# Where the block sums of V are made and turned, in an attention and expert kernel

## Chip, cores and metric

The kernel runs on one core of one Trainium2 chip. The metric is the device time of one execution in microseconds. A core has five engines with instruction streams of their own: TensorE (PE, with its weight loads as PEld), VectorE (DVE), ScalarE (ACT), GpSimd (POOL) and SyncE (SP, which issues most DMAs here). They meet only at semaphores.

## What is computed

The input x has 8 batches of 512 tokens with 256 features. It is layer-normalised to xn, and the output is x + attention(xn) + experts(xn). All is float32. The attention, cut to its core (16 heads, 16 features each):

```python
q, k, v = (xn @ Wq.T, xn @ Wk.T, xn @ Wv.T)      # split into 16 heads
qf, kf = taylor_exp(q), taylor_exp(k)            # [1, x / 16**.25, (x outer x) / (sqrt(2) * 4)]
A = jnp.tril(jnp.einsum('bhnd,bhmd->bhnm', qf, kf))
y = jnp.einsum('bhnm,bhme->bhne', A, v)
z = 1.0 / (jnp.einsum('bhld,bhld->bhl', qf, jnp.cumsum(kf, axis=2)) + EPS)
return (y * z[..., None]).reshape(b, l, 256) @ Wo.T
```

The experts are 8 feed-forward nets (256 to 512 and back, silu gate), of which each token uses the best two.

## The kernel before

**Scores.** With s = q.k, the score qf.kf is 1 + s/4 + s*s/32, which is ((s/4 + 1)^2 + 1) / 2. So TensorE makes s, and ScalarE makes the square (0.25 s + 1)^2 (`squares0`, `squares1`, `squares2`, lines 520 to 540). The 1 that is still to be added under the square gives, for a query, the sum of V over all keys up to it. The kernel gets it in two parts: inside a block of 128 tokens GpSimd masks the square with a fill of -1 (`mask`, line 476), and for blocks as a whole TensorE adds up V: that is the step C (lines 1088 to 1097), whose sums ScalarE copies to Cs (562) and TensorE turns (transposes) to columns, the step T (1098 to 1100); VectorE keeps them in CT (766) and adds them to each quad's product in `copy_yw` (719). V has a 17th column of ones, which gives the denominator in the same way.

**Quads.** The attention runs over 32 quads n = 4b + qd: batch b, four heads each. A quad has three parts of scores, and TensorE's program around them (lines 1149 to 1160) stands below with the lists. `attend(n - 1)` is the product of the last quad's squares with V (line 1056), made behind the first scores of this quad. `slot_a`, `slot_b` and `slot_c` (42 to 75) are lists written out by hand of the other steps that TensorE takes behind the first scores and the product, behind the second scores, and behind the third; ScalarE and VectorE walk the same lists for their share of each step. The steps:

- ("x", b, j): turn of xn (line 1067); ("c", b, k): a q product for k = 0 and 2 or a k product for k = 1 and 3 (1076), the "third q product" being c with k = 2, the q of quads 2 and 3 of the batch; ("v", b, j): V and router logits (1085)
- ("C", b, 0): block sums; ("T", b, 0): their turn
- ("t", b, qd): turn of a quad's product (1105), which VectorE then divides (`normalise`, 722 to 735, three instructions, the last of which, yn at 733, releases the bank)
- ("y", b, k): turn of yn (1111), k = 1 of which needs the t of quads 2 and 3; ("o", b, k): product with Wo (1120); ("r", b, 0): ranks of tokens for the experts (1125, 1127); ("f", ...): filler.

**Banks.** All these steps share three PSUM banks in rotation. `misc_uses` gives bank i % 3 to the i-th step of the whole list, and TensorE's `free` waits before a step until the step three places ahead of it in the list has been released by its last reader:

```python
    for i, key in enumerate(steps + list(END)):
        used[i % 3] += 1
        table[key] = (i % 3, used[i % 3])
```

For c with k = 2 the last reader is VectorE (744): ScalarE first copies the product to the high part of Q2 (553), then VectorE subtracts that copy from the bank for the low part and releases it. For c with k = 3 ScalarE copies K2 (555) and VectorE makes Kt (752). For y ScalarE copies yTh (568), VectorE makes yTl (775). For C the release is ScalarE's copy of Cs, for T VectorE's copy of CT.

**VectorE's order.** In its loop (959 to 973) a quad has copy_yw, the steps of slot_a, `before_b`, the steps of slot_b, `after_b`, the steps of slot_c, `after_c`. Line 966 puts the c of slot_b last on VectorE in quads 0 and 2, other than in the last batch. For quad 0 `before_b` is the gates of the experts, `after_b` the norm of the next batch's x.

**Moves.** The low and high parts of q and k go to other partitions by DMAs: `move_q` and `move_k` on SP's queue (lines 308 to 320, 349 to 365), four DMAs each, in a fixed order. The moves of q for quads 2 and 3 of a batch wait for c with k = 2, those of k behind them for c with k = 3. The scores of quads 2 and 3 wait for them (1029, 1030).

After quad 31 the expert stage runs 71 tiles of 128 gathered tokens (from line 1166).

Of the kernel before, what the change touches and what calls it, by code (L numbers as in the profile page):

```python
# [21 lines left out]
LAST = NBATCH - 1  # L22
# [18 lines left out]

def slot_a(n):

    return [("C", 0, 0)] if n == 0 else []


def slot_b(n):

    b, qd = divmod(n, 4)
    if qd == 0:  # L50
        steps = [("T", b, 0), ("c", b, 2)]
    elif b == LAST:
        steps = [("o", b - 1, qd - 1)] if qd < 3 else []
    elif qd == 1:
        steps = [("x", b + 1, 0), ("x", b + 1, 1)]
    elif qd == 2:
        steps = [("c", b + 1, 1)]
    else:
        steps = [("o", b - 1, 0)] if b else []
    if n == NQ - 1:  # L60
        steps.append(("f", n, 7))
    return steps + ([("t", (n - 1) // 4, (n - 1) % 4)] if n else []) + ([("G", 0, 0)] if n == NQ - 1 else [])


def slot_c(n):


    b, qd = divmod(n, 4)
    if qd == 0:
        return [("c", b, 3)] + ([("y", b - 1, 1)] if b else []) + [("r", b, 0)]  # L70
    if b == LAST:
        return [("y", b, 0)] if qd == 3 else [("f", n, 9)]
    if qd == 3:
        return ([("o", b - 1, 1)] if b else []) + [("y", b, 0), ("C", b + 1, 0)]
    return ([("c", b + 1, 0)] if qd == 1 else []) + [("v", b + 1, 2 * qd - 2), ("v", b + 1, 2 * qd - 1)]


# [35 lines left out]
def build(nc, x, wqk, wv, wo, w12, w3, out):  # L113
    with ExitStack() as ctx:
# [541 lines left out]
        def vector_program(e):  # L656
# [57 lines left out]
            def copy_yw(n):  # L714
                e.wait_ge(s["p_av"], n + 1)
                if n >= 2:
                    e.wait_ge(s["p_t"], n - 1)
                done(e, "T", n // 4, 0)
                e.tensor_tensor(yw[n % 2].rearrange("p (i m) -> p i m", i=4), banks[:, 4, :].rearrange("p (i m) -> p i m", i=4),
                                CT[:, n % 4, :].unsqueeze(2).to_broadcast([P, 4, P]), ALU.add).then_inc(s["v_yw"], 1)  # L720
# [199 lines left out]
            def after_b(n):  # L920
                b, qd = divmod(n, 4)
                if n == NQ - 3:
                    tile_starts()
                elif n == NQ - 2:
                    tile_rows(1)
                elif n == NQ - 1:
                    expert_ends()
                elif n == 0:
                    gates(0)
                elif qd == 0 and b < LAST:  # L930
                    norm_x(b + 1)
                elif qd == 1 and b < LAST:
                    place_rows(b)
                if n == NQ - 2:
                    w12_low(8)
# [23 lines left out]
            for n in range(NQ):  # L959
                if n:  # L960
                    copy_yw(n - 1)
                for item in slot_a(n):
                    step(*item)
                before_b(n)
                items = slot_b(n)
                if n % 4 in (0, 2) and n // 4 < LAST:
                    items = [i for i in items if i[0] != "c"] + [i for i in items if i[0] == "c"]
                for item in items:
                    step(*item)
                after_b(n)  # L970
                for item in slot_c(n):
                    step(*item)
                after_c(n)
# [265 lines left out]
        with nc.Block() as block:  # L1239
            block.sync(sync_program)  # L1240
            block.gpsimd(gpsimd_program)
            block.scalar(scalar_program)
            block.vector(vector_program)
            block.tensor(tensor_program)
# [34 lines left out]
```

## Time and profile before

| | |
|---|---|
| median of 3 runs | 668.18 us (668.07 to 668.24) |
| span of the profiled execution | 665.4 us |
| own time of the profiled execution | not listed, only its span |
| TensorE busy | 641.8 us, 96% |
| VectorE, ScalarE, GpSimd busy | 410.6, 341.6, 344.1 us |
| quads of the attention | about 20 to 301 us |

The span runs from the first to the last instruction; the run's time has some microseconds around it. "Busy" of TensorE means that a matmul was in flight. The granted clock is what the chip allowed TensorE, in tenths of full speed (2.4 GHz).

In a timeline each row has the start and the length in us, the engine, the line of the code, the instruction with out<-in, its shape and count, and in brackets the idle time before it with what ended it. Neighbouring matmuls overlap in their rows, since each row counts until its results have left the array.

### The profile page before, as it was taken

To read this page: it belongs to the slowest core of one execution; us is meant where nothing else is said; L and a number is where in the kernel's file an instruction comes from. 1 tells how busy PE (TensorE), PEld (TensorE's weight loads), DVE (VectorE), ACT (ScalarE), POOL (GpSimd) and SP (SyncE) were. 2 spreads that over 40 slices of the span, in tenths; PEclk is the share of its full clock that TensorE was granted. 3 is DMA by queue.
4 is the path that set the end of the run, shared out by engine and by line. 5 is a ranking of instruction groups with operands and counts; after the bars stand their busy time and mean duration, and the time that the engine had idled before them with its cause. 6 is when DMAs were issued, how large, how long until landed. Compare 5 with 4: busy or idle time off the path is not lost.

```text
span 665.4 us, 16423 instructions
## 1 busy us (share of the span) xinstructions
PE 641.8 (96%) x5414; PEld 496.5 (75%) x5414; DVE 410.6 (62%) x1067; ACT 341.6 (51%) x515; POOL 344.1 (52%) x381
## 2 busy tenths in 40 slices
PE   8899999999999999999999999999999999999994
PEld 7555666666666666657888888888888888888883
DVE  6777788787878585777975444444544445444452
ACT  3668878787877686766642232322323223232331
POOL 3265655546463736473465555455545555455542
PEclk9999999999999999999999999999999999999998
DMA  4653555554443435447633434333333433333332
GB/s 134 141 133 99 127 153 130 152 130 147 93 136 77 128 85 154 118 150 249 207 59 58 66 51 66 50 57 60 58 59 50 66 51 57 58 51 58 58 50 25
DMA packets 37775, 64.07 MB, mean 96 GB/s; under 512 B 8289, under 2 KB 25825, under 8 KB 37697
## 3 DMA queue, kind: packets, MB, share of 16 engines
q0 software_dynamic: 16704, 28.12, 22.0%
q1 hardware_dynamic: 20432, 34.24, 20.2%
q8 instruction: 50, 0.82, 0.5%
q10 hardware_dynamic: 560, 0.66, 0.3%
q14 instruction: 29, 0.23, 0.1%
HBM read 27.72 MB, written 22.68 MB: 76 GB/s over the span
## 4 chain that ended last, share of the span: by engine, by line
PE 87%; DVE 4%; DMA 2%; ACT 2%; issue 2%; SPq 1%; ACTq 0%; POOL 0%; POOLq 0%; DVEq 0%
PE banks L1182 29%; PE banks L1203 15%; PE banks L1056 10%; PE banks L1038 8%; PE banks L1076 7%; PE banks L1191 5%; PE banks L1085 4%; PE banks L1120 3%; PE banks L1171 2%; PE banks L1105 1%; PE banks L1111 1%; DMA K<-Kt 1%; ACT T L533 1%; DVE xTl L740 1%; PE banks L1094 1%
## 5 line engine op out<-in xcount | busy, mean ns | idle before, releaser
L496 POOL DMA_INDIRECT out<-yo,xw x71 | 112.2, 1581 | 154.4 <-DVE yo L996 76.6
L625 ACT ACTIVATE sTh<-banks 128x512 fp32r<-128x512 f32 x71 | 42.5, 598 | 192.4 <-PE banks L1191 186.6
L476 POOL TENSOR_SCALAR_AFFINE_SELECT T<-T 128x512 f32<-128x512 f32 x128 | 80.8, 642 | 108.5 <-ACT T L539 43.1
L988 DVE TENSOR_TENSOR sTl<-banks,sTh 128x512 fp32r<-128x512 f32 x71 | 49.0, 691 | 118.9 <-ACT sTh L625 118.9
L1182 PE MATMUL banks<-w12h,xgh 128*128 x284 | 118.0, 415 | 0.6 <-DVE xgl L979 0.6
L1182 PE MATMUL banks<-w12l,xgh 128*128 x284 | 112.2, 395 | 0.0
L1182 PE MATMUL banks<-w12h,xgl 128*128 x284 | 112.1, 395 | 0.0
L485 POOL DMA_INDIRECT xg<-xs_scr,glist x71 | 72.4, 1020 | 21.5 <-issue 20.0
L1056 PE MATMUL banks<-T,vau 128*17 128x512 f32 (+3 forms) x1024 | 75.6, 434 | 0.9 <-POOL T L476 0.9
L467 POOL DMA_INDIRECT xs_scr<-xb,slots x64 | 64.3, 1004 | 18.7 <-issue 10.0
L1038 PE MATMUL banks<-Q,K 32*128 32x256 f32 (+2 forms) x1024 | 70.5, 358 | 3.5 <-DMA K<-Kt 2.2
L525 ACT ACTIVATE T<-banks 128x1024 f32<-128x1024 f32 x64 | 62.1, 1026 | 12.5 <-PE banks L1038 11.9
L533 ACT ACTIVATE T<-banks 128x768 f32<-128x768 f32 x64 | 48.5, 810 | 27.2 <-PE banks L1038 27.2
L1182 PEld LDWEIGHTS banks<-w12h,xgl 128*128 128x128 f32 x284 | 53.3, 188 | 12.0
L1056 PEld LDWEIGHTS banks<-T,vau 128*17 128x17 f32 x1024 | 26.0, 97 | 46.3 <-issue 38.4
L1182 PEld LDWEIGHTS banks<-w12h,xgh 128*128 128x128 f32 x284 | 53.8, 189 | 7.8 <-issue 1.0
L1038 PEld LDWEIGHTS banks<-Q,K 32*128 32x128 f32 x1024 | 38.6, 183 | 27.1 <-ACT T L525 12.7
L1182 PEld LDWEIGHTS banks<-w12l,xgh 128*128 128x128 f32 x284 | 53.9, 190 | 6.3
L996 DVE TENSOR_SCALAR yo<-banks,xw 128x256 f32<-128x256 f32 x71 | 34.3, 483 | 39.0 <-PE banks L1203 31.2
L539 ACT ACTIVATE T<-banks 128x768 f32<-128x768 f32 x64 | 48.7, 810 | 18.0 <-PE banks L1038 16.1
L1009 DVE TENSOR_TENSOR hs<-banks,hs 128x512 f32<-128x512 f32 x71 | 49.1, 692 | 10.2 <-PE banks L1182 0.9
L1203 PE MATMUL banks<-w3h,sTh 128*128 x284 | 51.1, 302 | 0.8 <-ACT sTh L625 0.8
(174 smaller groups left out, 1222.3 us busy)
## 6 DMA issues: line engine op xcount, KB each, us to landing
Q<-Q SPq DMA_DIRECT2D x128, 64.0 KB, 2.4
w12r<-w SPq DMA_DIRECT2D x16, 512.0 KB, 4.2
out<-xa SPq DMA_DIRECT2D x16, 256.0 KB
w3r<-w SPq DMA_DIRECT2D x8, 512.0 KB, 8.7
K<-Kt SPq DMA_DIRECT2D x124, 32.0 KB
xa<-x SPq DMA_DIRECT2D x7, 512.0 KB, 4.7
xg<-xs_scr,glist POOLq DMA_INDIRECT x71
out<-yo,xw POOLq DMA_INDIRECT x71
```

What stands on the lines that cost most here:

```text
L467: e.indirect_dma_start(xs_d, bass.IndirectOffsetOnAxis(slots[:, k, 4 * b + blk:4 * b + blk + 1].bitcast(U32), 0), xb[b % 2][:, blk, :], No ...
L476: e.affine_select(out=v, in_=v, pattern=[[0, 4], [1, P]], compare_op=ALU.is_ge, fill=-1.0, base=0, channel_multiplier=-1).then_inc(s["g_mk ...
L485: e.indirect_dma_start(xg[:, t % GR, :], None, xs_d, bass.IndirectOffsetOnAxis(glist[:, t:t + 1].bitcast(U32), 0)).then_inc(s[f"d_g{t % GR ...
L496: e.indirect_dma_start(out, bass.IndirectOffsetOnAxis(xw[:, t % 4, NE:NE + 1].bitcast(U32), 0), yo[:, t % 2, :], None, compute_op=ALU.add) ...
L525: e.activation(T0[n % 2][:, 2 * h:2 * h + 2, :], banks[:, 2 * h:2 * h + 2, :], ACT.Square, scale=0.25, bias=1.0).then_inc(s["a_s"], 1)
L533: e.activation(T1[:, 2 * h:2 * h + 2, :], banks[:, 2 * h:2 * h + 2, 0:384], ACT.Square, scale=0.25, bias=1.0).then_inc(s["a_s"], 1)
L988: e.tensor_tensor(sTl[:], banks[:, 5, :], sTh[:].bitcast(F32), ALU.subtract).then_inc(s["v_st"], 1)
L1009: e.tensor_tensor(hs[:], banks[:, 2 * (t % 2) + 1, :], hs[:], ALU.mult).then_inc(s["v_mu"], 1)
L1038: i = e.matmul(banks[:, r, c0:c0 + w], K2[rr, g, h, jm * P:(jm + 1) * P], Q2[g][rr, h, p, 512 - w:512], start=(p == 0), stop=(p == 1))
L1056: i = e.matmul(banks[32 * r:32 * r + HA, 4, 512 - w:512], vau[b % 2][:, jm, 4 * qd + r, :], v[:, r, :], start=(jm == 0), stop=(jm == 2), s ...
L1182: i = e.matmul(banks[:, 2 * (t % 2) + m, :], a[:, k, :], w[:, bass.ds(expert[t] * 4 + (2 * k + m), 1), :], start=(k == 0 and n == 0), stop ...
L1203: i = e.matmul(banks[:, 6 + t % 2, 0:256], a[:, k * P:(k + 1) * P], w[:, bass.ds(expert[t] * 4 + k, 1), :], start=(k == 0 and n == 0), sto ...
```

## The change

In slot lists: C of a batch goes from slot_c of the quad before to slot_a of its own quad 0; behind it, c with k = 2 goes ahead of T in slot_b. On VectorE the c of quad 0 is no longer put last. The bank rotation follows the new order by itself. Nothing else is changed.

```diff
 def slot_a(n):
-    return [("C", 0, 0)] if n == 0 else []
+    return [("C", n // 4, 0)] if n % 4 == 0 else []

 def slot_b(n):
     b, qd = divmod(n, 4)
     if qd == 0:
-        steps = [("T", b, 0), ("c", b, 2)]
+        steps = [("c", b, 2), ("T", b, 0)]
...
 def slot_c(n):
...
     if qd == 3:
-        return ([("o", b - 1, 1)] if b else []) + [("y", b, 0), ("C", b + 1, 0)]
+        return ([("o", b - 1, 1)] if b else []) + [("y", b, 0)]
...
                 items = slot_b(n)
-                if n % 4 in (0, 2) and n // 4 < LAST:
+                if n % 4 == 2 and n // 4 < LAST:
                     items = [i for i in items if i[0] != "c"] + [i for i in items if i[0] == "c"]
```

## Rows read from the trace of the kernel before

**Rows 1.** The page: busy time by engine, and TensorE's granted clock in 40 slices
```profile
PE 641.8 (96%) x5414; PEld 496.5 (75%) x5414; DVE 410.6 (62%) x1067; ACT 341.6 (51%) x515; POOL 344.1 (52%) x381
...
PEclk9999999999999999999999999999999999999998
```

**Rows 2.** The list of waits of TensorE: us in total, times, longest us
```profile
engine line waited for: us in total, times, longest us
PE banks L1076 <- DVE xTl L740: 3.6, 7, 0.5
...
PE banks L1038 <- DMA K<-Kt: 2.2, 2, 1.4
```

**Rows 3.** Timeline of TensorE at batch 4: start, length, engine, line, instruction, idle before
```profile
158.46 0.68 PE L1094 MATMUL banks<-vau,below 128*32 128x68 f32 x32
...
159.07 0.74 PE L1038 MATMUL banks<-Q,K 32*128 32x512 f32 x8
...
159.73 2.35 PE L1056 MATMUL banks<-T,vau 128*17 128x512 f32 x32
...
162.01 0.62 PE L1038 MATMUL banks<-Q,K 32*128 32x384 f32 x8
...
162.57 0.33 PE L1100 MATMUL banks<-ident,Cs 128*128 128x128 f32 x1
...
162.65 0.48 PE L1076 MATMUL banks<-xTh,Wqh 128*128 128x512 f32 x1
...
165.33 0.50 PE L1076 MATMUL banks<-xTh,Wqh 128*128 128x512 f32 x1
...
166.59 0.39 PE L1076 MATMUL banks<-xTl,Wqh 128*128 128x512 f32 x1
...
166.87 0.66 PE L1111 MATMUL banks<-ident,yn 128*128 128x128 f32 x4
```

**Rows 4.** Timeline of ScalarE at batch 4
```profile
156.83 1.57 ACT L539 ACTIVATE T<-banks 128x768 f32<-128x768 f32 x2 [1.55 <-PE banks L1038]
...
159.20 0.23 ACT L562 ACTIVATE Cs<-banks 128x68 f32<-128x68 f32 x1
...
159.84 1.94 ACT L525 ACTIVATE T<-banks 128x1024 f32<-128x1024 f32 x2 [0.40 <-PE banks L1038]
...
162.67 1.51 ACT L533 ACTIVATE T<-banks 128x768 f32<-128x768 f32 x2 [0.80 <-PE banks L1038]
...
164.32 1.03 ACT L553 ACTIVATE Q<-banks 128x1024 fp32r<-128x1024 f32 x1
```

**Rows 5.** Timeline of VectorE at batch 4
```profile
165.60 1.21 DVE L744 TENSOR_TENSOR Q<-banks,Q 128x1024 fp32r<-128x1024 f32 x1
```

**Rows 6.** Timeline of TensorE at batch 1: the first scores, the product behind
```profile
53.10 1.11 PE L1038 MATMUL banks<-Q,K 32*128 32x512 f32 x8
...
54.14 2.35 PE L1056 MATMUL banks<-T,vau 128*17 128x512 f32 x32
```

**Rows 7.** Timeline of ScalarE at batch 7: the copy of Q
```profile
269.82 1.03 ACT L553 ACTIVATE Q<-banks 128x1024 fp32r<-128x1024 f32 x1
```

**Rows 8.** Timeline of VectorE at batch 7, and at quad 30
```profile
270.88 1.22 DVE L744 TENSOR_TENSOR Q<-banks,Q 128x1024 fp32r<-128x1024 f32 x1 [1.11 <-ACT Q L553]
...
273.57 0.69 DVE L752 TENSOR_TENSOR Kt<-banks,K 128x512 fp32r<-128x512 f32 x1 [0.65 <-ACT K L555]
...
274.37 0.69 DVE L775 TENSOR_TENSOR yTl<-banks,yTh 128x512 fp32r<-128x512 f32 x1
...
285.65 0.69 DVE L719 TENSOR_TENSOR yw<-banks,CT 128x512 f32<-128x512 f32 x1 [0.44 <-PE banks L1056]
```

**Rows 9.** Timeline of VectorE at batch 0
```profile
26.71 1.22 DVE L744 TENSOR_TENSOR Q<-banks,Q 128x1024 fp32r<-128x1024 f32 x1 [1.24 <-ACT Q L553]
```

**Rows 10.** Timeline of TensorE at batch 0: the scores behind r
```profile
27.92 0.94 PE L1038 MATMUL banks<-Q,K 32*128 32x512 f32 x8
```

**Rows 11.** Timeline of TensorE at batch 7: y1
```profile
273.07 0.63 PE L1111 MATMUL banks<-ident,yn 128*128 128x128 f32 x4 [0.59 <-DVE yn L733]
```

## The prediction

> **What bounds the kernel now.** I read the page first: TensorE is busy for 96% of a 665.4 us span and its granted clock is full in all but the last slice [rows 1]. So what matters is where TensorE waits, and what a new wait would cost. The list of waits gives only a few: 3.6 us in seven pieces of 0.5 us on xTl, and 2.2 us in two pieces on the moved K rows [rows 2]. Then I read the timelines of one joint between two batches, quad 16 (batch 4, quad 0), engine by engine. On TensorE the block sums take from 158.46 to 159.07, 0.61 us, then come the first scores, the product with V, the second scores at 162.01, the turn of the sums (162.57), the third q product c2 (162.65), the turn of y, the third scores, the k product c3 (165.33 to 166.59 for its last matmul) and the turn y1 at 166.87 [rows 3]. There is no gap anywhere but in front of y1: c3's six matmuls come 0.25 us apart, so y1 could have started at 166.84 and waited about 0.03. ScalarE makes the high part of Q at 164.32, behind the second squares (162.67 plus 1.51, so until 164.18) [rows 4]. VectorE makes the low part of Q from 165.60 to 166.81 [rows 5], and y1 starts 0.06 us behind it: y1 uses the PSUM bank that c2 had.
>
> The three banks are handed round by the order of the list, so each step waits for the release of the step three places before it. Now the order is y0, C, T, c2, t, c3, y1, r: c3 waits for T (long free) and y1 for c2. With the change it is y0, C, c2, T, t, c3, y1, r: **c3 waits for c2**, y1 for T. That is the step on which this forecast stands: the release of c2 is VectorE's subtraction L744, and it is late.
>
> **The change part by part.** (a) C moved from behind y0 to behind the product with V, in seven batches (batch 0 has it there already). Its matmuls stay the same, 0.61 us [rows 3]; the first scores and the product start 0.61 us earlier, C fills the place, and the second scores start at 162.01 as before. The trace has C only between other neighbours, so its price there is unknown. Its row is 0.68 us long and lies over the next one for 0.07 of it: without that overlap it costs 0.07 more, with twice the overlap 0.07 less; I take 0, the row as it is. ScalarE's copy of the sums now falls between the squares: the first squares end at 159.84 plus 1.94 less 0.61, 161.17, C ends at about 162.07, the copy lasts 0.23 us and the exponent of four columns behind it, as I estimate from that, no longer, the second squares start at 162.67 [rows 4]. It fits with some 0.1 us to spare. If that cover were gone it would cost up to that 0.45 us a batch; I count 0 and leave it for the upper end.
>
> (b) The cover at the joint. C gave ScalarE time to finish the last squares of the quad before. The first scores of row groups 2 and 3 wait for them. At batch 1 they wait already: scores start at 53.10 and take until 54.14, 1.04 us [rows 6], where batch 4 takes 0.66 (159.07 to 159.73) [rows 3]. With C gone from in front they start at 52.49 and still end at 54.14, and C comes on top behind the product: **0.61 us** lost once. In batch 4 the last squares are through at 156.83 plus 1.57, 158.40 [rows 4], against a new start of the scores at 158.46, and the other batches look like it: 0, or at the most 0.1 us each.
>
> (c) c2 ahead of T. T took 0.08 us ahead of c2 (162.57 to 162.65) [rows 3], so the Q copy can start at 164.32 less 0.08, 164.24, the squares being through at 164.18. In batch 7, where VectorE had nothing else to do, subtraction follows the start of the copy by 270.88 less 269.82, 1.06 us [rows 7, 8]. So: subtraction 165.30 to 166.51, c3 0.06 later at 166.57, where it started at 165.33: a new wait of 1.24 us. y1 then comes 1.51 us behind (six matmuls) at 168.08 against 166.87: **1.21 us** a batch. The other steps behind c3 hold no wait that could give this back: the xTl waits [rows 2] come from scores, squares and transposes that all move with TensorE. T on TensorE costs about 0.13 behind c2 (a quarter of the turn of y), hidden in the new wait. Batches 1 to 6: 6 x 1.21 = 7.3 us.
>
> (d) VectorE: c, T, t in place of T, t, c. The subtraction cannot start before the Q copy ends, and T, the reciprocals and yn of t queue behind it on that engine; y1 needs yn and could start at 167.59 by the pace of batch 7 (worked out with the first rival). That is before 168.08, so this wait is hidden behind the one of (c). The norm of the next x and Kt come later by less than the 1.21 us by which TensorE is late, so who reads them doesn't notice. (e) The queue of SP: Q moves wait for the subtraction, which ends 0.3 us earlier; eight Q moves stand before the K moves, so the later Kt costs nothing. At batches 0 and 7, where TensorE waits for moved K rows [rows 2], this gives back 0.06 to 0.1 us each. No DMA is added or dropped.
>
> (f) Batch 0: no y1, but r takes c2's bank. The subtraction ends at 26.71 plus 1.22, less 0.08 [rows 9], so r starts at about 27.91, where its scores start at 27.92 now [rows 10]: r, of five small matmuls, is some 0.2 us late. Its scores already lose 0.2 us or so to the squares (a row of 0.94 against one of 0.74 in batch 4); so 0, at most 0.2. (g) Batch 7 has c, then t on VectorE now, and y1 waits for yn there, until 273.07 [rows 11]. c3 can start at 270.88 plus 1.22 [rows 8], at 272.1 or so, y1 at 273.61, 0.54 late. c3's end is 272.1 plus 1.26 plus 0.39 (rows 3's last matmul), 273.75; the copy of K takes 1.03 like that of Q [rows 7], so Kt starts at 274.83, not 273.57, and yTl behind it at 275.44, not 274.37: VectorE is 1.07 us late [rows 8]. From there it shows no idle until the copy of yw at 285.65, which had 0.44 us to spare [rows 8], and none behind that up to the lists of the gathers. TensorE's own lateness disappears in its wait for K rows (the shorter of rows 2), but VectorE's 1.07 less 0.44 stays: **0.65 us**; the ends are 0.1 (TensorE alone counts) and 1.1.
>
> Sum: 0 + 0.61 + 7.3 + 0.65, less 0.1 for (e) = 8.4 us, against the profiled span of 665.4, so a span of 673.8. Around a span lie 668.18 less 665.4, 2.8 us, which stay: 676.6 us. The page gives no time of the profiled execution besides its span, so the sum is made against the span and set on the median, whose runs lie within 0.2 us of each other. The expert stage is untouched.
>
> **The rivals.** *Only yn is waited for* (673.2 us). If the bank wait of c3 did not bite, y1 would wait for yn. Batch 7 has nearly that order now: from subtraction to y1 2.19 us [rows 8, 11]; with T's small copy between them I take 0.1 more (between 0 and the 0.2 of the smallest copies), so y1 at 165.30 plus 2.29, 167.59, 0.72 later than now. Six times 0.72, plus 0.61 and 0.1: 5.0 us. Against it stands the rotation as written in the code, and that y1 waits for c2's bank now. *Not slower* (668.4 us): if the C step's earlier place let ScalarE's Q copy run so early that VectorE's subtraction ended before TensorE reaches c3, both waits would be gone, with y1's 0.03 a batch and the earlier Q moves (0.1 at batches 0 and 7) as a gain, 0.4 us, against the 0.61 of batch 1. It decides at 165.33: the subtraction would have to end by then, so the copy to start by 163.06. The second squares, which stand before it on ScalarE, only start at 162.67 and take 1.51 [rows 4]; nothing in the rows makes them earlier. *ScalarE's chain breaks* (679 us): the copy of the sums holds up the second squares by 0.3 us or more in seven batches; above the forecast by 2.1 to 3.
>
> *The clock falls.* TensorE would then stand still seven times for 1.24 us. Its longest wait now, 1.4 us [rows 2], is followed by a full granted clock, and the clock is below full only in the last slice, where TensorE has no work [rows 1]. If the scores and the product behind each new wait (2.94 us at 2.4 GHz, 159.07 to 162.01 [rows 3]) ran at 1.2 GHz, that would be 7 x 2.94 = 21 us more, 697 us. The Trainium skill, "TensorE: Matmul & The Clock Gate", section "A second HAM failure mode: psum-queue depth-cycling", says that short idles between groups of matmuls that cycle through PSUM banks can make the clock swing between its levels; by that rule 697 us would come out, and the trace, with waits of 0.5 to 1.4 us and no drop, so far speaks against it.
>
> **How the numbers follow.** The forecast of c3's wait 0.86; only yn 0.05; ScalarE's chain 0.04; the clock 0.01; not slower 0.04 (0.01 of it for a gain larger than I can name). The range is the forecast's own: low, the six batches at 1.0 and no joint or tail, 668.2 + 6.1 = 674.3; high, 1.3 in six batches, 0.61, 1.1 and a little for C's new neighbours, 678.2. It leaves the yn case outside, and holds the smaller breaks of ScalarE's chain in part. About 0.2% (1.3 us) is what a measurement of this kernel can tell from no change; slower by more 0.96, within 0.03, faster 0.01.
>
> **What would show it.** In the list of waits c3 (L1076) waits on VectorE's Q (L744), seven times, about 1.2 us each; y1 no longer waits; C (L1094) stands behind L1056; at batch 1 scores take about 1.6 us. If c3 follows the third scores with no gap, the forecast is wrong; if the gap is before y1 and named yn, it is the first rival; if the second squares start over 0.1 us after the first half of their scores, ScalarE's chain broke; a granted clock below 1.00 behind the waits is the last.

## The result and the profile after

The changed kernel takes 678.26 us (median of 4 runs, 677.41 to 678.54) and the kernel before 668.21 us (median of 4, 668.07 to 669.03) on the same chip: a ratio of 1.0146 [1.0132, 1.0159]. That is 10.05 us more. 676.6 was forecast, with 674.3 to 678.2 as the range, so the sign and the mechanism came out as forecast, the size was 1.7 us too small, and the median lies 0.06 us above the upper end. The profiled execution of the changed kernel took 677.41 us, with a span of 675.7 us (665.4 before), so 1.7 us lie around a span here.

The page of the changed kernel, busy time and TensorE's granted clock:

```profile
PE 643.3 (95%) x5414; PEld 499.6 (74%) x5414; DVE 409.8 (61%) x1067; ACT 341.2 (50%) x515; POOL 344.1 (51%) x381
...
PEclk9999999999999999999999999999999999999998
```

No engine is busier than in [rows 1] but TensorE, by 1.5 us, and the clock is as before. So the 10 us of this profile are nearly all waits. The other three executions took 678.00 to 678.54 us and have a mean granted clock of 0.991 to 0.994, where this one has 0.996. The list of waits of TensorE says which (us in total, times, longest us):

```profile
PE banks L1076 <- DVE Q L744: 8.8, 7, 1.5
PE banks L1076 <- DVE xTl L740: 3.6, 7, 0.5
PE banks L1038 <- ACT T L525: 1.4, 3, 0.5
...
PE banks L1038 <- DMA K<-Kt: 1.2, 1, 1.2
...
PE banks L1125 <- DVE Q L744: 0.8, 1, 0.8
```

The first row is new: seven waits of a k product (L1076) for VectorE's subtraction of Q (L744), the ones forecast. y1 (L1111) has no row of its own. The xTl waits are those of [rows 2] to the tenth, and the K rows are waited for once, not twice. The same joint as in [rows 3], TensorE at batch 4:

```profile
163.83 0.74 PE L1038 MATMUL banks<-Q,K 32*128 32x512 f32 x8
164.50 2.35 PE L1056 MATMUL banks<-T,vau 128*17 128x512 f32 x32
166.66 0.66 PE L1094 MATMUL banks<-vau,below 128*32 128x68 f32 x32
167.25 0.62 PE L1038 MATMUL banks<-Q,K 32*128 32x384 f32 x8
167.80 0.50 PE L1076 MATMUL banks<-xTh,Wqh 128*128 128x512 f32 x1
...
169.29 0.27 PE L1100 MATMUL banks<-ident,Cs 128*128 128x128 f32 x1
...
171.90 0.50 PE L1076 MATMUL banks<-xTh,Wqh 128*128 128x512 f32 x1 [1.23 <-DVE Q L744]
...
173.40 0.60 PE L1111 MATMUL banks<-ident,yn 128*128 128x128 f32 x4
```

C (L1094) stands behind the product (L1056), c2 (167.80) ahead of T (169.29), and the only gap is the 1.23 us ahead of c3 (171.90). ScalarE and VectorE in the same stretch, beside [rows 4] and [rows 5]:

```profile
167.38 0.24 ACT L562 ACTIVATE Cs<-banks 128x68 f32<-128x68 f32 x1 [0.84 <-PE banks L1094]
167.51 0.20 ACT L572 ACTIVATE gx<-gx 128x4 f32<-128x4 f32 x1
167.90 1.51 ACT L533 ACTIVATE T<-banks 128x768 f32<-128x768 f32 x2 [0.20 <-issue]
169.49 1.03 ACT L553 ACTIVATE Q<-banks 128x1024 fp32r<-128x1024 f32 x1
```

```profile
170.62 1.23 DVE L744 TENSOR_TENSOR Q<-banks,Q 128x1024 fp32r<-128x1024 f32 x1 [1.63 <-ACT Q L553]
171.76 0.16 DVE L766 COPY CT<-banks 128x16 f32<-128x16 f32 x1
...
172.33 0.42 DVE L733 TENSOR_TENSOR yn<-banks,rd 128x256 f32<-128x256 f32 x1
```

The copy of the sums and the exponent fit between the squares with 0.2 us to spare. VectorE stood idle for 1.63 us before the subtraction, for it can't start before ScalarE's copy of Q; the subtraction ends at 171.84 or so, and c3 starts 0.06 behind. yn is ready before c3 is through.

**Where the time went.** I take the start of the first scores in the last quad of each batch, in the changed kernel's profile less that of the kernel before (all worked out from the timelines of TensorE):

```
last quad of batch      0     1     2     3     4     5     6     7
later than before    0.84  3.29  4.35  5.45  6.47  7.51  8.84  10.03 us
added by the batch   0.84  2.45  1.06  1.10  1.02  1.04  1.33   1.19
```

Batches 2 to 6 add 5.55 us, 1.11 each. Batch 1 adds 2.45 and batch 7 adds 1.19. The other 0.84 was there by the last quad of batch 0, and 0.27 comes behind quad 31 (10.3 in all). The forecast had 0 for batch 0, 1.82 for batch 1, 5 x 1.21, 6.05, for batches 2 to 6, 0.65 for batch 7 and 0 behind it, less 0.1.

### The profile page after: what moved, and what is told of

It is laid out like the page before. It is cut to its first block, busy times and chain, and to the rows that moved or that the text cites. A ratio compares the mean times of both kernels' runs of the same rounds, so it can differ in the third digit from the quotient of the medians.

```text
span 675.7 us, 16430 instructions
## 1 busy us (share of the span) xinstructions
PE 643.3 (95%) x5414; PEld 499.6 (74%) x5414; DVE 409.8 (61%) x1067; ACT 341.2 (50%) x515; POOL 344.1 (51%) x381
## 4 chain that ended last, share of the span: by engine, by line
PE 86%; DVE 5%; ACT 4%; issue 2%; DMA 1%; POOL 0%; POOLq 0%; DVEq 0%; ACTq 0%
PE banks L1182 29%; PE banks L1203 15%; PE banks L1056 10%; PE banks L1038 8%; PE banks L1076 7%; PE banks L1191 4%; PE banks L1085 4%; PE banks L1120 4%; PE banks L1171 2%; DVE Q L744 2%; ACT Q L553 1%; PE banks L1105 1%; ACT T L533 1%; PE banks L1111 1%; DVE xTl L740 1%
## 5 line engine op out<-in xcount | busy, mean ns | idle before, releaser
L496 POOL DMA_INDIRECT out<-yo,xw x71 | 114.5, 1613 | 154.1 <-DMA out<-yo,xw 66.1
L485 POOL DMA_INDIRECT xg<-xs_scr,glist x71 | 70.9, 999 | 21.5 <-issue 20.9
L1056 PE MATMUL banks<-T,vau 128*17 128x512 f32 (+3 forms) x1024 | 75.6, 434 | 1.0 <-POOL T L476 1.0
L525 ACT ACTIVATE T<-banks 128x1024 f32<-128x1024 f32 x64 | 62.1, 1026 | 10.3 <-PE banks L1038 9.2
L1056 PEld LDWEIGHTS banks<-T,vau 128*17 128x17 f32 x1024 | 25.9, 97 | 46.3 <-issue 40.4
```

What stands on the lines that cost most here:

```text
L485: e.indirect_dma_start(xg[:, t % GR, :], None, xs_d, bass.IndirectOffsetOnAxis(glist[:, t:t + 1].bitcast(U32), 0)).then_inc(s[f"d_g{t % GR ...
L496: e.indirect_dma_start(out, bass.IndirectOffsetOnAxis(xw[:, t % 4, NE:NE + 1].bitcast(U32), 0), yo[:, t % 2, :], None, compute_op=ALU.add) ...
L525: e.activation(T0[n % 2][:, 2 * h:2 * h + 2, :], banks[:, 2 * h:2 * h + 2, :], ACT.Square, scale=0.25, bias=1.0).then_inc(s["a_s"], 1)
L1056: i = e.matmul(banks[32 * r:32 * r + HA, 4, 512 - w:512], vau[b % 2][:, jm, 4 * qd + r, :], v[:, r, :], start=(jm == 0), stop=(jm == 2), s ...
```

## Experiments

All kernels compute everything. Their times are compared with the kernel before in the same series of runs on the same chip: its median was 668.59 us in the first series, 668.46 in the second, 666.69 in the third and 668.49 in the fourth.

### Which edit makes the wait

The change consists of four things: C's place, c2 ahead of T on TensorE, c ahead of T and t on VectorE, and, through the order of the list, the bank that each step gets. First C alone, T and VectorE's order as before.

```diff
-        steps = [("c", b, 2), ("T", b, 0)]
+        steps = [("T", b, 0), ("c", b, 2)]
...
-                if n % 4 == 2 and n // 4 < LAST:
+                if n % 4 in (0, 2) and n // 4 < LAST:
```

> Only C is moved: T stays ahead of c2 and VectorE's order is that of before, so c3's bank is again T's. Theory (the bank wait of c3 makes the loss): the 1.2 us waits of c3 are gone in all batches; what is left is the joint at batch 1 (0.61 less the 0.12 us by which C is cheaper behind the product, 0.5) and 6 x 0.12 = 0.7 us gained at batches 2 to 7: 668.0 us, between 667.4 and 669. Rival (moving C itself makes the loss, by its place on TensorE or by ScalarE's copy between the squares): 674 or more. Side bet: T now stands directly behind the second scores and needs the copy of C's sums, so if ScalarE's copy is late at batch 1, as it is by 1.3 us in the changed kernel's profile, TensorE waits there about 1 us.

Measured: 670.06 us (12 runs), ratio 1.0016 [1.0001, 1.003]. That is 1 us above the range, far below the rival's 674. The waits of c3 for L744 are gone from its list of waits, and one of 1.1 us is new, at batch 1, as the side bet had it:

```profile
PE banks L1100 <- ACT Cs L562: 1.1, 1, 1.1
```

So C's place is not what costs 10 us. Then the changed kernel with only VectorE's order set back (T, t, c):

```diff
-                if n % 4 == 2 and n // 4 < LAST:
+                if n % 4 in (0, 2) and n // 4 < LAST:
```

> The changed kernel, but with VectorE's order T, t, c in quad 0 as before. c2 stays ahead of T on TensorE, so c3 still takes c2's bank. Theory: in batch 4 yn would end near 170.9 on the changed kernel's clock and the subtraction start there and not at 170.62, so c3 waits about 0.25 us longer per batch: slower than the changed kernel by 6 x 0.25 to 7 x 0.3 us, 679.8 us (679 to 681). Rival (it is VectorE's new order, yn behind the subtraction, that costs): faster than the changed kernel, near 673.

Measured: 679.86 us (5 runs), ratio 1.0167 [1.0139, 1.0195]:

```profile
PE banks L1076 <- DVE Q L744: 10.0, 7, 1.5
```

The wait is longer, 1.43 us each in place of 1.26, since the subtraction now has yn ahead of it on VectorE: 1.47 in batches 2 to 6 in place of 1.23, the 0.25 that was expected. In batch 7 it is 1.22 in both, for there line 966 leaves VectorE's order as it is. So the bank alone makes the wait, with either order. The third kernel keeps VectorE's new order and swaps the banks of c2 and T, so that c3 waits for T's release, as before:

```diff
         table[key] = (i % 3, used[i % 3])
+    for b in range(NBATCH):
+        table["c", b, 2], table["T", b, 0] = table["T", b, 0], table["c", b, 2]
```

> The changed kernel in every order, but c2 and T have their PSUM banks swapped, so that c3 takes T's bank and y1 takes c2's, as before. Theory: c3 no longer waits, but now the wait that it hid comes out: y1 waits for yn, which stands behind the subtraction and T's copy on VectorE. y1 comes 2.19 + 0.1 us behind the start of the subtraction (172.9 and not 173.40 in batch 4), 0.5 us a batch earlier: 675.0 us (674 to 676). Rival (the bank wait was the whole loss): 669 or less. Rival (bank not involved): 678.

Measured: 678.99 us (5 runs), ratio 1.0147 [1.0122, 1.0173]: no better than the changed kernel. This expectation was wrong. (Its profile has a fall of the clock at batch 1, shown with the rivals below. Batches 2 to 6, where the clock is full, add 5.8 us, and 5.55 in the changed kernel.) VectorE and then TensorE at batch 4 of this kernel (in it and in the fourth kernel all lines are 2 higher, so CT is L768 and c3 L1078):

```profile
173.39 1.23 DVE L746 TENSOR_TENSOR Q<-banks,Q 128x1024 fp32r<-128x1024 f32 x1 [1.63 <-ACT Q L555]
174.53 0.16 DVE L768 COPY CT<-banks 128x16 f32<-128x16 f32 x1
```

```profile
174.75 0.50 PE L1078 MATMUL banks<-xTh,Wqh 128*128 128x512 f32 x1 [1.30 <-DVE CT L768]
```

c3 now waits for the copy CT. That is a 0.16 us step, but it stands directly behind the subtraction on VectorE, and so comes as late. A bank is released when its reader gets its turn, not when the reader's own work would allow it. The fourth kernel makes both edits; C's place and c2 ahead of T on TensorE stay.

> Banks swapped and VectorE's order T, t, c back; C's new place and c2 ahead of T on TensorE stay. Theory: both waits are gone, y1 waits at most 0.05 us for c2's bank; per batch 1.25 us less than in the changed kernel; left are the joint at batch 1 (0.5) and C's cheaper place (-0.12 a batch): 668.2 us (667.5 to 669.2). Rival (C's place or c2 ahead of T on TensorE has a price of its own): 670 or more.

Measured: 670.55 us (12 runs), ratio 1.0023 [1.0006, 1.004]. That is above the expected 667.5 to 669.2 and in the rival's reach (670 or more). c3 waits once (list of waits, then timeline of TensorE):

```profile
PE banks L1078 <- DVE CT L768: 1.3, 1, 1.3
```

```profile
275.02 0.50 PE L1078 MATMUL banks<-xTh,Wqh 128*128 128x512 f32 x1 [1.30 <-DVE CT L768]
```

That is batch 7. Line 966 never put the c of the last batch behind T, before or after the change, so VectorE has c, T, t there also in this kernel: with T's bank that is the third kernel, and the wait is the third kernel's. VectorE shows why c3 doesn't wait at batch 4:

```profile
167.64 0.17 DVE L768 COPY CT<-banks 128x16 f32<-128x16 f32 x1 [0.66 <-PE banks L1102]
...
168.86 1.21 DVE L746 TENSOR_TENSOR Q<-banks,Q 128x1024 fp32r<-128x1024 f32 x1
```

CT is copied 1.2 us before the subtraction starts. The last three kernels and the changed one are a table of two by two: with the subtraction ahead of the release that c3 waits for, by the bank, by VectorE's order or by both, 1.0146 to 1.0167; with neither, but for batch 7, 1.0023. This is most of the loss of the change. In the profile of the fourth kernel batch 1 adds 0.93 us, batch 7 with its wait 1.07, and batches 2 to 6 take off 0.54. c2's place ahead of T on TensorE was not run by itself; what it could cost lies within these numbers.

### What C's move costs and gives by itself

Starts of the first scores in the last quad of each batch, later than in the profile of the kernel before, in us (worked out from the timelines; the first row is mostly the start-up, which differs from profile to profile):

```
batch   C alone   C alone   C alone,     C alone,     before,
                  from 2    20 waits     60 waits     60 waits
0         0.95     1.74       1.97         0.17         1.95
1         2.73     1.77       2.59         0.78         1.96
2         2.66     1.84       2.32         0.94         2.22
4         2.49     1.53       1.68         0.36         2.18
6         2.11     1.12       1.12        -0.06         2.34
7         2.47     0.79       0.51        -0.69         3.17
```

The second column leaves C of batch 1 where it was:

```diff
-    return [("C", n // 4, 0)] if n % 4 == 0 else []
+    return [("C", n // 4, 0)] if n % 4 == 0 and n != 4 else []
...
-        return ([("o", b - 1, 1)] if b else []) + [("y", b, 0)]
+        return ([("o", b - 1, 1)] if b else []) + [("y", b, 0)] + ([("C", 1, 0)] if b == 0 else [])
```

> Only the block sums are moved, and only in batches 2 to 7; batch 1 keeps them behind y0 in the last quad of batch 0. T stands ahead of the third q product on TensorE and on VectorE, as in the kernel before. My theory: the step C is about 0.12 us cheaper behind the product with V than behind y0, in every batch, and what the kernel with only C moved lost it lost at batch 1 (its joint, 0.61, and a pause of ScalarE ahead of the copy of the sums, about 1 us). So here: the scores of quad 4 and 5 start as in the kernel before within 0.2 us (start-up differences of the runs apart), from quad 8 on they come earlier by 0.12 a batch, about 0.6 us in all, and the time is 667.3 to 668.2 where the kernel before has 668.5: ratio about 0.999. The rival: the gain per batch is a matter of chance in the profiles, and the time is the kernel before's, ratio 1.000 with its interval on both sides. A second rival: the pause of ScalarE (2.3 us between the end of the first squares and the copy of the sums) belongs to the first time that this order of steps is met, not to batch 1; then it shows at batch 2 and costs 0.6 to 1 us there.

Measured: 667.96 us (12 runs), ratio 0.9997 [0.9977, 1.0016]. Batch 1 adds 0.03 in place of 1.78. From batch 2 to 6 the lead grows by 0.65 us, 0.13 a batch (0.62 with C alone). In the rows: from the product to the second scores [rows 3] have 162.01 less 159.73, 2.28 us, with C elsewhere, and C cost 0.61 ahead of the first scores; behind the product C begins 2.16 us after the product (166.66 less 164.50) and the second scores 0.59 later, so the two cost 2.75 and not 2.89. The gain is in every profile with C moved and not in the last column. But that column, in which nothing but the 60 waits differs from the kernel before, drifts by 0.38 us from batch 1 to 6 and by another 0.83 in batch 7 (there TensorE waits 1.67 us for K rows in place of 0.85). So a few tenths in these tables are differences between executions, and 0.6 us is below what the runs can tell. The second rival fell: batch 2 shows no pause.

The joint of batch 1 was forecast at 0.61. C alone loses 1.78 there. The rest is a pause of ScalarE between the end of its first squares and the copy of the sums, here in the changed kernel:

```profile
54.87 1.94 ACT L525 ACTIVATE T<-banks 128x1024 f32<-128x1024 f32 x2
59.10 0.23 ACT L562 ACTIVATE Cs<-banks 128x68 f32<-128x68 f32 x1 [2.29 <-PE banks L1094]
```

2.29 us, where the other batches have 0.84, although TensorE's row of C ends in time for it:

```profile
57.14 0.66 PE L1094 MATMUL banks<-vau,below 128*32 128x68 f32 x32
57.73 0.62 PE L1038 MATMUL banks<-Q,K 32*128 32x384 f32 x8
```

57.80, and 1.30 us pass until the copy. The trace's semaphore events (no view lists them) say that it is not ScalarE that pauses, but TensorE's signals that come late: the signal of the block sums at 59.08, 1.28 us behind their last row, and the two signals of the second scores at 59.15 and 59.20, 0.8 behind theirs. In batches 2 to 7 the signal of the block sums comes 0.04 behind their rows, in every profile. In the kernel before it is late at batch 1 as well, and only there, by 0.44 us.

Before the runs below I took the pause for a reload of ScalarE's instructions that falls there, and moved its stream by 15 instructions:

```diff
-            e.wait_ge(s["d_wqk"], 16)
+            for _ in range(16):
+                e.wait_ge(s["d_wqk"], 16)
```

> The block sums are moved in all batches and T stays where it was, as in the second experiment's sibling with C alone; besides, ScalarE's program starts with 15 more waits on a semaphore that is long set by then, which cost next to nothing and move all its later instructions by 15 places in its stream. At batch 1 ScalarE pauses 2.3 us ahead of the copy of the sums in every profile with C moved, and in no other batch (0.84). My theory: the pause is a reload of ScalarE's instructions that falls at this place of its stream. Then here it falls elsewhere: the copy of the sums at batch 1 follows the first squares after about 0.84 us, the 1.1 us wait for it ahead of T is gone, and the time is 0.5 to 1.0 us below that of the kernel with only C moved (670.1), 669.1 to 669.5, unless the pause lands on another step that TensorE waits for. The rival: the pause is a wait that the work itself causes at batch 1 (late squares, a late transfer); then it stays, 2.3 us, and so does the time.

> This is the changed kernel itself with the same 15 additional waits at the start of ScalarE's program. By my theory the pause ahead of the copy of the sums at batch 1 (2.29 us) shrinks to about 0.84, the copy of Q there is 0.7 us earlier, the third q product's successor c3 waits 1.2 us at batch 1 instead of 1.5 and its scores of quad 5 start 0.7 us earlier, and the time is 0.3 to 0.8 us below the changed kernel's, 677.5 to 678.0. The rival, a cause in the work of batch 1: nothing changes, 678.3.

Measured: with C alone 673.56 us (6 runs), ratio 1.0064 [1.0046, 1.0083], the whole change 679.48 us (5 runs), 1.0161 [1.014, 1.0182]. The times don't bear on the question, for the waits were not as free as I wrote: ScalarE loads its table behind them and not ahead, and its first copy of weights waits for that.

```profile
8.90 1.28 ACT L584 ACT_TABLE_LOAD   x1 [8.90 <-DMA wqk_r<-wqk]
```

The first scores come 4.7 and 3.2 us later than before. But the pause itself is 2.26 us in both profiles, so it isn't ScalarE's place in its stream. TensorE's was next, with 20 and with 60 waits ahead of its first scores, where it waits for K rows:

```diff
                 step(*item)
+            for _ in range(20):
+                e.wait_ge(s["c_id"], 1)
             for n in range(NQ):
```

> The kernel with only the block sums moved, with 20 more waits on TensorE on a semaphore that is long set, between its first steps and the first scores, where TensorE waits for moved K rows anyway (some 20 x 0.05 us, hidden). The shift on ScalarE left the 2.3 us pause ahead of the copy of the sums at batch 1 where it was, so it is not ScalarE's own stream. Open: is it TensorE's? In the trace the signal of the block sums comes about 1.25 us behind their last matmul at batch 1 (0.05 to 0.3 elsewhere), while the matmuls behind it keep their pace. Theory: that delay depends on the place in TensorE's stream of instructions, so with 20 more ahead of it the copy of the sums at batch 1 follows the squares after about 0.84 us, the 1.1 us wait of T is gone, and the scores of quad 5 come 0.8 to 1.1 us earlier than in the kernel with only the sums moved. The rival: it is the work of batch 1 itself, and the pause stays at 2.2 to 2.3 us.

> The same with 60 more waits (3.1 us, still inside TensorE's wait for K rows or over it by under 1 us). If the place in TensorE's stream decides, the pause at batch 1 is gone here or in the run with 20, and may turn up behind another step; if the pause stays in both at 2.2 to 2.3 us, the cause lies in the work of batch 1 and remains unnamed.

Measured: 666.6 us, 0.9999 [0.9986, 1.0011], and 666.98 us, 1.0003 [0.9986, 1.0019] (10 runs each). The pause is 1.18 us with 20 (its row below) and 1.19 with 60, T waits no more, and batch 1 adds 0.62 and 0.61 us, about the joint as forecast. The signal is 0.17 to 0.18 us late in these two.

```profile
59.12 0.23 ACT L562 ACTIVATE Cs<-banks 128x68 f32<-128x68 f32 x1 [1.18 <-PE banks L1094]
```

That looked like the answer. Two controls were to settle it: the kernel before and the changed kernel, each with the 60 waits.

> The kernel before with nothing but the 60 more waits on TensorE between its first steps and the first scores. With them the kernel with only the sums moved came to 1.0003 [0.9986, 1.0019] of the kernel before, where without them it had 1.0016. Theory: the shift by itself gives the kernel before nothing that can be measured (no signal of its TensorE steps is seen late at batch 1), 0.999 to 1.001, and it loses or gains under 0.5 us at the start of quad 4. The rival: the place in the stream is worth something at other steps as well; then this one is faster than before by 0.5 us or more, and what the kernel with the sums moved gained by the shift was not its pause at batch 1.

> The changed kernel with the 60 more waits on TensorE. Theory: the pause at batch 1 goes (2.3 to about 1.2 us), c3 there waits about 1.2 us instead of 1.5, the scores of quad 5 come 0.7 to 1.0 us earlier against the changed kernel, the other six waits stay at 1.2 to 1.3 us, and the time is 0.5 to 1.0 us under the changed kernel's: 1.013 to 1.014 of the kernel before instead of 1.0146. The rival: the c3 wait hides the pause, and nothing changes.

Measured: before 669.82 us (12 runs), 1.0021 [1.0006, 1.0037], above the expected 0.999 to 1.001 (in its profile the clock falls at the start, see the last section), changed 677.07 us (6 runs), 1.0134 [1.0107, 1.0161]. The second number lies where it was expected, but by luck, for what was to bring it there did not happen: the changed kernel has its pause again, with the same 60 waits on TensorE:

```profile
61.21 0.23 ACT L562 ACTIVATE Cs<-banks 128x68 f32<-128x68 f32 x1 [2.24 <-PE banks L1094]
```

and batch 1 adds 2.41 us, as without them. Its ratio is lower than the changed kernel's by less than its interval. So the place in the stream doesn't explain it either. The two profiles without the pause come from the one series in which the kernel before, too, ran 1.8 us faster than in the others, and in which C alone without the waits was not run; what differed there, I can't tell. It is not the chip, for the last series ran on the same one. Those two traces also hold 30 and 32 of the 32 signals of VectorE's yw, all others 16 to 26, so the recording of the trace may have a part in it; that is not shown. **The pause stays open**: it is 2.24 to 2.29 us in all nine profiles of the other series with C of batch 1 moved, with the signal 1.23 to 1.28 us behind the matmuls' rows.

### What stays late in batch 7

The forecast named VectorE. In the profile of the changed kernel VectorE reaches the copy of yw of quad 30 and has to wait for TensorE, so it has caught up:

```profile
295.43 0.69 DVE L719 TENSOR_TENSOR yw<-banks,CT 128x512 f32<-128x512 f32 x1 [0.51 <-PE banks L1056]
```

ScalarE has not. Behind the late c3 it makes the copy of K, that of y and the high part of a w12 piece without a gap, and the squares of quad 29 start 1.91 us behind their first scores (284.91 less 283.00), where before it was 1.44 (275.18 less 273.74); TensorE waits for them:

```profile
282.57 1.02 ACT L555 ACTIVATE K<-banks 128x1024 fp32r<-128x1024 f32 x1 [1.37 <-PE banks L1076]
283.49 0.59 ACT L568 ACTIVATE yTh<-banks 128x512 fp32r<-128x512 f32 x1
283.97 1.06 ACT L576 ACTIVATE w12h<-w12r 128x1024 fp32r<-128x1024 f32 x1
284.91 1.94 ACT L525 ACTIVATE T<-banks 128x1024 f32<-128x1024 f32 x2
```

```profile
286.91 0.61 PE L1038 MATMUL banks<-Q,K 32*128 32x384 f32 x6 [0.47 <-ACT T L525]
```

The first scores of quad 30 then take 1.34 us in place of 0.74, because the squares of quad 29 are not through. The fourth kernel, whose only wait of c3 is the one of batch 7, bears out that this belongs to the wait: there quad 29 starts 1.11 us later against quad 28 than in the kernel before, and quad 31 0.85 later against quad 30; in the changed kernel it is 1.03 and 0.84, with C alone 0.47 (C's own time) and 0.22. To see whether it is the w12 step that leaves ScalarE without slack, I moved it one quad on:

```diff
-W12_WITH = {(1, 1): 0, ..., (4, 2): 7, (7, 0): 8}
+W12_WITH = {(1, 1): 0, ..., (4, 2): 7, (7, 1): 8}
```

> This is the changed kernel with one step of ScalarE moved by one quad: the high part of the last of the nine w12 pieces is made beside quad 1 of batch 7 instead of quad 0. In the profile of the changed kernel that step (283.97) stands ahead of the first squares of a quad in which ScalarE comes late, and the scores behind it wait for the squares. My theory: what batch 7 loses beyond the forecast (about 1.0 us measured as a later start of its last quads) is ScalarE's, not VectorE's; with the step moved, the start of quad 31's scores against the kernel before is 9.5 us or less late instead of 10.0, and the time is 0.3 to 0.8 us below the changed kernel's, 677.4 to 678.0. The rival, the prediction's own (VectorE is what stays late in batch 7): no difference, 678.3 within 0.3.

Measured: 681.48 us (5 runs, 678.78 to 682.52), ratio 1.0171 [1.0146, 1.0196]. The total went the other way, and both theories were too simple. Later than before, quads 29, 30 and 31 start by 9.26, 9.19 and 10.03 us in the changed kernel and by 11.63, 10.35 and 11.89 here, where the run as a whole is 2.36 behind it at quad 28. From quad 28 to 30 that is -0.25 where the changed kernel has +0.95: without the w12 step ScalarE catches up, as I held. But there it was only moved, so quad 31 starts 1.29 later than quad 28 did, for 1.79 (0.50 gained). And its low part, on VectorE, now came at a bad moment. VectorE was busy without a gap from 289.59 on, and TensorE stood before the turn of yw:

```profile
305.24 1.22 DVE L706 TENSOR_TENSOR w12l<-w12r,w12h 128x1024 fp32r<-128x1024 f32 x1
...
308.49 0.69 DVE L719 TENSOR_TENSOR yw<-banks,CT 128x512 f32<-128x512 f32 x1
```

```profile
309.32 0.63 PE L1105 MATMUL banks<-ident,yw 128*128 128x128 f32 x4 [2.48 <-DVE yw L719]
```

So in batch 7 ScalarE was the late one, and VectorE, which the forecast named, stood close behind. Then the clock fell. The stretches of this profile (us, busy time and instructions of PE, PEld, DVE, ACT and POOL, granted clock, share of DMA, GB/s):

```profile
306.00:308.00 2.00, 0.85 (x7) 0.61 (x6) 1.93 (x4) 1.51 (x2) 1.95 (x2) 1.00 0.24 89
308.00:310.00 2.00, 0.68 (x9) 0.54 (x9) 1.12 (x4) 0.00 (x0) 1.62 (x2) 1.00 0.28 104
310.00:312.00 2.00, 2.00 (x25) 1.40 (x28) 1.57 (x5) 1.23 (x2) 0.00 (x0) 0.66 0.01 4
312.00:314.00 2.00, 2.00 (x12) 0.34 (x8) 1.13 (x2) 1.98 (x3) 1.42 (x3) 0.50 0.02 4
```

TensorE works for 1.5 us of four, and the granted clock then goes from its level of 2.4 GHz to that of 1.2 for 3 us or so, with TensorE full. The span grew by 5.0 us over the changed kernel's, while quad 31 was only 1.9 us later; the other 3.1 are these waits and this clock.

## Why the prediction was right, and where not

**Right: the bank.** c3 waits for c2's subtraction, seven times, 8.8 us in all, and the runs with banks and order taken apart show that nothing else in the change makes a loss of that size. From the second scores the copy of Q was forecast 2.23 us behind (164.24 less 162.01), measured 2.24 (169.49 less 167.25); the subtraction 3.29, measured 3.37; c3 4.56, measured 4.65; y1 1.51 behind c3, measured 1.50. The wait is 1.23 for 1.24.

**Step (a), C at 0 or 0.07 either way:** C is 0.12 to 0.14 cheaper behind the product, outside that bound. With it a batch adds 1.11 and not 1.21, 0.5 us less in batches 2 to 6.

**Steps (b) and (c) at batch 1, forecast 1.82, measured 2.45.** The joint is 0.61: the first scores and the gap ahead of them take from 53.39 to 54.98, 1.59 us, as "about 1.6" said. What was missing is ScalarE's pause, that is the late signal of the block sums. By it the copy of Q comes late, c3 waits 1.50 in place of 1.23, and the third scores take 1.20 in place of 0.74 (their squares are late too). 0.61 plus 1.50 plus 0.46 less 0.12 is 2.45. No row of before shows it, though its semaphore events have that signal 0.44 us late at batch 1; and the cover of 0.1 us in (a) was argued from batch 4 alone; a sum for seven batches wants each batch's own slack, or a wider upper end.

**Step (d)** held: yn is never waited for, and yn's wait of 0.59 us in batch 7 [rows 11] is gone.

**Steps (e) and (f).** TensorE waits for K rows once and not twice. Batch 0 is 0.84 us later, where 0 to 0.2 was forecast. The profile with C alone, whose batch 0 is that of the kernel before, has 0.95 there, 0.63 of it behind its first scores, so this is mostly a difference between executions and not the change. In both, two small steps of VectorE (L790, L796) run beside a mask of GpSimd and take 0.51 to 0.59 us in place of 0.19 and 0.16; the exponent waits for the second, and ScalarE's copy of Q stands behind the exponent, at 26.26 in the changed kernel in place of 25.65. r (L1125) then waits 0.8 us for L744, by its row, because it has c2's bank; "at most 0.2" left no room for a late copy of Q.

**Step (g), forecast 0.65, measured 1.19.** TensorE's 1.2 us of lateness did partly vanish in the wait for K rows, and VectorE had the slack that was worked out. The step that failed is "VectorE's 1.07 less 0.44 stays": I followed VectorE and not ScalarE, whose chain behind c3 has no gap either and holds a w12 step. That was to be seen in the timeline of before, where the same four steps follow each other from 272.51 to the squares at 275.18, with 0.20 us of idle time among them.

**The sum.** The terms that were mis-sized are (b) with (c) at batch 1, (f) and (g). 8.4 became 10.3 between the spans: +0.84 of the start, +0.63 at batch 1, -0.5 in batches 2 to 6, +0.54 at batch 7, +0.27 behind quad 31 (the other profiles differ there as much), and 0.1 that (e) did not give back. The clock is in none of these, but the other three executions, at a lower mean clock than the profiled one, took 0.6 to 1.1 us more than it, and the median is one of theirs. The 2.8 us around the span were 668.18 less a span of another execution: wherever the record has both, they are 1.7 to 1.8. The prediction put its 8.4 us on the median, so this does not move 676.6.

**The rivals.** Only yn waited for: fell, y1 waits for nothing. Not slower: fell, the subtraction ends 1.2 us after c3 could start. ScalarE's chain: held with 0.2 us to spare (batch 4) in six batches and broke once, at batch 1. The clock: in the profile of the changed kernel it is full behind all seven waits of 1.2 to 1.5 us. But it did fall at batch 1 in two others, the third kernel behind a wait of 1.59 us and the changed kernel with ScalarE's stream moved behind one of 1.50. The third kernel (columns as in the table above, then the row of c3):

```profile
62.00:64.00 2.00, 0.45 (x14) 0.24 (x10) 1.32 (x3) 1.98 (x3) 0.44 (x1) 1.00 0.00 0
64.00:66.00 2.00, 1.96 (x5) 1.60 (x6) 1.93 (x6) 0.00 (x0) 1.22 (x2) 0.59 0.37 57
66.00:68.00 2.00, 2.00 (x15) 1.62 (x17) 0.67 (x3) 1.27 (x2) 0.00 (x0) 0.55 0.62 100
```

```profile
64.04 0.52 PE L1078 MATMUL banks<-xTh,Wqh 128*128 128x512 f32 x1 [1.59 <-DVE CT L768]
```

c3's matmuls come 0.43 us apart there in place of 0.23, and batch 1 adds 4.05 us, in the other profile 3.92, where it is 2.45 with a full clock. So one such fall costs some 1.5 us and not the 2.94 a batch of the prediction, and it came only at batch 1, in two of the six profiles that wait 1.4 to 1.6 us there. Behind the 37 waits of c3 in batches 2 to 7 of these profiles and the fourth kernel's, 1.2 to 1.5 us long, the clock stayed full. So 697 us did not come out, but the rival is real: the prediction's 0.01 was for the fall behind every wait, and a fall behind one of them was not priced. Whether it is in the three executions of the changed kernel without a profile is not known. By the rule of the Trainium skill ("TensorE: Matmul & The Clock Gate", section "A second HAM failure mode: psum-queue depth-cycling") the clock swings with such short idles; here it did so behind two of these 43 waits, and, in the run with w12 moved, behind a wait of 2.48 us with other gaps around it.

## What to carry to other kernels

- Where steps share banks in rotation by their place in a list, moving one step changes who waits for whom for all behind it. Write down, for each step near the move, which release it waits for before and after, and when the reader gets its turn: both the bank and the place in the reader's own queue count, and undoing one of the two bought nothing here (1.0147 and 1.0167 against 1.0146), undoing both bought 8 us. And look for the batch that the code treats otherwise: undoing both left the wait of the last batch in place.
- A lateness passed on to the other engines stays with the one that has no gap left. Follow each of them to its first idle time, not only the one that released late.

## What was not expected of the hardware

**The clock can fall at the start, whatever the kernel.** In ten of the fourteen profiles it is at its lower level once between 22 and 32 us, for 3.4 to 6.8 us; the profile of the kernel before with 60 waits is one of them. The page of the fourth kernel has 9 and then 7 in its first slices:

```profile
PEclk9799999999999999999999999999999999999998
```

and this is one stretch of it, with the columns of the last such table:

```profile
22.00:24.00 2.00, 1.28 (x30) 0.71 (x20) 1.83 (x9) 1.81 (x3) 0.16 (x1) 0.68 0.64 105
24.00:26.00 2.00, 2.00 (x9) 1.37 (x10) 1.70 (x8) 1.51 (x2) 0.47 (x1) 0.50 0.62 119
```

It follows TensorE's gaps between 20 and 24 us. The profile of the kernel before has such gaps too and a full clock. The runs of the kernel before with a mean granted clock of 0.990 took 669.2 to 670.3 us in the second series, those with 0.995 to 0.996 took 667.1 to 668.5. So the spread goes with the clock, and this fall is likely a large part of it (executions without a profile don't show where their clock fell). It is why half a microsecond can't be told here.

**Small instructions of VectorE stretch while GpSimd masks.** In the run with w12 moved:

```profile
291.52 0.71 DVE L831 TENSOR_TENSOR ge<-ge,tl 128x64 f32<-128x64 f32 x1
```

```profile
291.51 0.64 POOL L476 TENSOR_SCALAR_AFFINE_SELECT T<-T 128x512 f32<-128x512 f32 x1
```

The same instruction takes 0.23 us in the profiles of before and after, where no mask runs beside it. It ends with the mask, within 0.1 us. It is not this step alone: in the profile of the changed kernel, of the steps of VectorE that take up to 0.26 us at their shortest (lines with six or more of them), 30 of the 65 that start beside a mask take over 1.6 times that, and none of the 244 that start while GpSimd does nothing. So in batch 7, where VectorE has a long row of such steps, where the masks fall shifts the moment when it is through.
